# One mask product for both diagonal blocks of a bank of scores

## What is computed

```python
attn = jnp.einsum('bhqd,bhkd->bhqk', q, k) * scale
causal = jnp.triu(jnp.ones((Tc, Tc), dtype=bool), k=1)
attn = jnp.where(causal, -jnp.inf, attn)
attn = jax.nn.softmax(attn, axis=-1)
out = jnp.einsum('bhqk,bhkd->bhqd', attn, v)
```

```python
sim1 = jnp.einsum('bthd,hkd->bthk', q[..., 0, :], keys[:, :, 0, :])
s1, i1 = jax.lax.top_k(sim1, K)
fs, pk = jax.lax.top_k(all_sc, K)
hidden = jax.nn.gelu(jnp.einsum('btd,bthkd->bthk', xn, wd), approximate=False)
return jnp.einsum('bthk,bthkd->btd', hidden * jax.nn.relu(fs), wu)
```

## Time and profile before

| | us |
|---|---|
| median of 3 runs | 1625.49 |
| lowest and highest | 1624.69, 1626.40 |
| the profiled execution | 1626.17 |
| its span, first to last instruction | 1624.4 |
| granted TensorE clock, mean over the span | 0.904 |

### The profile page before, as it was taken

The page is one execution under the profiler, slowest core; times in us unless marked ns, Lnnn a source line. Parts: engine busy times, 40 slices in busy tenths (PEclk is TensorE's granted clock), DMA queues, the critical chain, the costliest instruction groups (busy, mean ns, idle before and its releaser), DMA issues.

```text
span 1624.4 us, 55167 instructions
## 1 busy us (share of the span) xinstructions
PE 1353.0 (83%) x21008; PEld 973.5 (60%) x21008; DVE 1358.7 (84%) x6568; ACT 926.0 (57%) x1502; POOL 665.0 (41%) x1024
## 2 busy tenths in 40 slices
PE   3567788989898998989898998989898988977567
PEld 3333456657575766667574766666575756655557
DVE  3314599999999898999999998999999998798984
ACT  0665766666675666666666766666666756442110
POOL 1412627171725436171826345270817355050410
PEclk9977899989898999989898999989898999998676
DMA  3000000000000000000000000000000000000000
GB/s 85 7 1 14 1 8 9 8 16 9 16 9 15 3 15 9 8 15 9 15 9 15 9 15 2 9 16 8 16 8 16 3 15 3 2 15 2 9 1 17
DMA packets 29989, 18.81 MB, mean 12 GB/s; under 512 B 1824, under 2 KB 29216, under 8 KB 29728
## 3 DMA queue, kind: packets, MB, share of 16 engines
q1 hardware_dynamic: 29728, 15.23, 3.3%
HBM read 11.04 MB, written 4.19 MB: 9 GB/s over the span
## 4 chain that ended last, share of the span: by engine, by line
PE 41%; DVE 36%; ACT 9%; issue 8%; POOL 5%; SPq 1%; DVEq 0%; DMA 0%; ACTq 0%; POOLq 0%
DVE onehot L1263 10%; PE G L938 7%; PE OV L827 7%; PE F L883 7%; DVE topi L1209 6%; PE G L927 6%; DVE psel L1225 4%; DVE whot L1288 3%; PE S L813 3%; DVE topv L1203 3%; ACT prob L631 3%; DVE fsel L1220 2%; DVE hid L1301 2%; PE S L753 2%; PE F L893 2%
## 5 line engine op out<-in xcount | busy, mean ns | idle before, releaser
L631 ACT ACTIVATE prob<-S 128x512 f32<-128x512 f32 x640 | 371.0, 596 | 146.7 <-PE S L815 140.4
L927 PE MATMUL G<-whot,onehot 128*128 128x16 bf16 x12288 | 383.5, 170 | 33.4 <-DVE hid L1301 19.6
L927 PEld LDWEIGHTS G<-whot,onehot 128*128 128x128 bf16 x12288 | 364.8, 97 | 68.2 <-issue 18.4
L1263 DVE TENSOR_TENSOR onehot<-lo_no,elo 128x1024 bf16<-128x1024 uint16 x512 | 386.4, 806 | 0.0
L827 PE MATMUL OV<-prob,vp 128*9 128x512 f32 (+3 forms) x2048 | 183.6, 508 | 67.9 <-ACT prob L631 62.0
L494 POOL TENSOR_TENSOR gat<-gat,cande 128x1280 f16<-128x1280 f16 x64 | 178.6, 2790 | 75.9 <-DVE gat L1231 75.9
L815 PE MATMUL S<-causal,ident_b 128*128 128x128 bf16 x1024 | 200.9, 229 | 0.0
L813 PE MATMUL S<-qT,kT_even 128*128 128x512 bf16 (+3 forms) x512 | 145.1, 312 | 53.7 <-ACT prob L631 45.0
L503 POOL COPY y<-y_new 128x512 f32<-128x512 f32 x16 | 9.8, 611 | 434.2 <-DVE r L1187 376.7
L563 ACT ACTIVATE hid<-F 128x512 f32<-128x512 f32 x128 | 76.6, 598 | 188.3 <-PE F L883 188.3
L827 PEld LDWEIGHTS OV<-prob,vp 128*9 128x9 f32 x2048 | 54.9, 99 | 198.2 <-issue 107.2
(11 more groups left out here) (134 smaller groups left out, 2498.7 us busy)
## 6 DMA issues: line engine op xcount, KB each, us to landing
xa<-in_L_attn_x SPq DMA_DIRECT2D x16, 256.0 KB, 2.9
xr<-in_L_attn_x SPq DMA_DIRECT2D x16, 256.0 KB, 3.0
out<-r SPq DMA_DIRECT2D x16, 256.0 KB, 2.3
onehot<-in_L_ffn_expert_down SPq DMA_DIRECT2D x1, 512.0 KB, 6.0
up<-in_L_ffn_expert_up SPq DMA_DIRECT2D x1, 512.0 KB, 6.6
onehot<-in_L_ffn_keys SPq DMA_DIRECT2D x1, 256.0 KB, 6.4
onehot<-in_L_attn_w_qkv SPq DMA_DIRECT2D x1, 192.0 KB, 4.4
onehot<-in_L_attn_w_proj SPq DMA_DIRECT2D x1, 64.0 KB, 4.7
```

Of the source, the lines that this page charges most:

```text
L631: act.activation(dst, src, ACT.Exp, scale=SCALE).then_inc(exp_done.sem, 1)
L927: last = nc.tensor.matmul(bank[:, 16 * i:16 * i + 16], onehot[:, row, :], whot[:, t, w_part, :], start=(w_part == 0), stop=(w_part == 2))
L1263: return dve.tensor_tensor(onehot[:, row:row + 8, :].rearrange("p t (c i) -> p t c i", i=2), lo, e, ALU.is_equal)
```

## The change

A unit with two blocks has one mask product where it had two. Both score products are issued first, and then one product of the identity with the mask, which is read twice (a step of 0 between the two readings), into the first 128 columns of both blocks (columns 0 and 256, or 0 and 384, of the bank). The second block's score product no longer has `start=True`. Units with one block keep their two products.

```diff
-                    for half, kc, col in SCORES[u % 5]:
+                    blocks = SCORES[u % 5]
+                    for half, kc, col in blocks:
+
                         pe_k = kT[half][:, j, kc * P:(kc + 1) * P]
                         nc.tensor.matmul(bank[:, col:col + T - kc * P], pe_k, qT[:, j, kc * P:T],
-                                         start=True, stop=False, skip_group_check=True)
-                        last = nc.tensor.matmul(bank[:, col:col + P], ident_b[:, :], causal[:, :],
-                                                start=False, stop=True, skip_group_check=True)
-                    last.then_inc(s_ready.sem, 1)
+                                         start=(col == 0), stop=False, skip_group_check=True)
+
+                    if len(blocks) == 2:
+                        diagonal = bank[:, :].rearrange("p (c n) -> p c n", n=P)[:, 0:NT:blocks[1][2] // P]
+                        mask = causal[:, :].unsqueeze(1).to_broadcast([P, 2, P])
+                    else:
+                        diagonal, mask = bank[:, 0:P], causal[:, :]
+                    nc.tensor.matmul(diagonal, ident_b[:, :], mask, start=False, stop=True, skip_group_check=True)\
+                        .then_inc(s_ready.sem, 1)
```

## The result

| | before | after |
|---|---|---|
| median, us | 1625.79 (4 runs) | 1649.70 (4 runs) |
| lowest and highest | 1624.69, 1626.40 | 1647.96, 1650.79 |
| ratio after to before | | 1.0147, 95% interval 1.0129 to 1.0164 |
| profiled execution, and its span | 1626.17, 1624.4 | 1648.66, 1646.9 |

The forecast was 1625.2 us in a range of 1620.5 to 1629.0. The kernel lost 24 us.

The account below looks back on a forecast made before the run. Neither PE nor DVE alone was taken to bound the kernel; they share the chain (41% and 36%). 128 merged masks on the chain at 2.5 ns save 0.3 us from the 1625.49 us median, giving 1625.2 us, range 1620.5 to 1629.

Parts of the forecast that it names:

- the part on the merged masks: PE's mask products in 384 two-block units: 384 products and 384 loads go, while the columns stay.
- Merged mask, 2.5 ns each, 0.3 us in all: Two-block units on the chain, 8 per iteration over sixteen iterations: 128 x 2.5 ns = 0.3 us less.
- The order and the start flag: First mask moved behind the second block's scores, and that score product with start=False: neither costs anything.
- ACT's waits: ACT waiting for the last mask's semaphore: 140.4 us in 254 of 640 cases, expected to stay near 140 us.
- The new form of the mask: Merged mask's repeated reading and split output: 0.11 us taken, bounded by 7 us won and 18 us lost.
- Rival A: PE's operand loads are partly exposed where the chain passes: up to 12.5 us less, 1613 us; chance 4%.
- the 81 ns per pair: Skill's spacing of load and product pairs at 128 columns: each merged pair saves 64 ns, 8 us less in all.
- Rival B: PE takes the merged mask's new form at half the rate: 14 us more, 1639 us; chance 10%.
- Its own sign: Rival B's mark in the profile after: a distance of 0.14 us or more behind a merged mask.
- Rival C, the clock's pattern: PE's clock falls at other moments in the iterations: 1620.6 or 1627.7 us; chance 7% faster, 2% slower.
- the forecast's sign of 90.0 to 90.7 us: Loop iterations should stay between these lengths; a move of 0.3 us or more would mean another clock pattern.
- The range's lower end: Rival C's fast end of 1620.6 us less the 0.3 us gain, some 1620.5 us.

Follow-up runs that it names:

- after_dead145: Changed kernel with 148 more instructions ahead of the loop, a branch over 145 never-executed semaphore increments: 1621.59 us, 0.9976 of the kernel before.
- order_alone: Kernel before with the change's product order and start flag, but still two masks of 128 columns per unit: 1621.65 us, 0.9993 of the kernel before.
- after_shift145: Changed kernel with 145 executed empty semaphore increments at the start of PE's list, none in the loop: 1625.69 us, 1.0026 of the kernel before.
- before_dead61: Kernel before, its masks untouched, shifted by 64 instructions that are never executed: 1636.39 us, 1.0065 of the kernel before.
- before_shift64: Kernel before, its products untouched, with 64 executed empty semaphore increments at the start of PE's list: 1630.62 us, 1.0052 of the kernel before.
- before_dead7: Kernel before, shifted by 10 instructions that are never executed: 1668.41 us, 1.0269 of the kernel before.
- after_dead253: Changed kernel shifted by 256 instructions in all that are never executed: 1648.21 us, 1.0136 of the kernel before.

## Why the prediction was wrong

**The step that failed** is the first sentence of the part on the merged masks and what was made of it: "384 products and 384 loads go" was priced by the time that they take in a stream. Their absence also moved everything behind them in the list, by 144 instructions at the loop's head and 192 at its back branch. The forecast put this at nothing, without a term or a reason for it, and called the clock the only way by which 0.3 us could grow. What the runs showed in its place: with the positions restored the merged mask costs nothing (0.9996), and with positions like the changed kernel's the untouched kernel is 0.5 to 1% slower. The missing term was 2.5 us at each of eleven back branches, 27.6 us in all, less what the exit no longer costs. That the positions are the cause is shown; how the fetch is timed is the theory.

**What a row could have told.** The chain before held "issue" at 8% of the span, and its longest piece at the loop's exit was 3.42 us ahead of the attention product, with 0.20 to 0.26 us at each back branch. I took these for a matter of the loop, not for a price that depends on how many instructions there are. The page before showed 16.4 KB per instruction transfer, and the count of instructions up to the branch can be had from a built program without a run. The stop right behind the exit said where an edge lies. Together these rows could have told that the branch would land early in a block, but not what that costs.

**Point by point.**
- *Merged mask, 2.5 ns each, 0.3 us in all*: right as far as it can be told. The unit still takes 0.33 us, and with the branch in its old place the whole is 0.9996 of before. The loop's eleven iterations, 994.55 us before, are as long in after_dead145:

```profile
sum 994.59, PE 869.70 PEld 639.56 DVE 919.90 ACT 636.86 POOL 464.15; mean PE 79.06 PEld 58.14 DVE 83.63 ACT 57.90 POOL 42.20
```

- *The order and the start flag, nothing*: right (order_alone).
- *ACT's waits*: 136.6 us in 247 cases in place of 140.4 in 254, as forecast.
- *The new form of the mask*, bounded between 7 us won and 18 lost and taken at 0.11 us: right, it costs what a plain product of 256 columns costs.
- *Rival A, and the 81 ns per pair that the Trainium skill gives at 128 columns* (TensorE: Matmul & The Clock Gate, section Back-to-back issue gap): nothing of it shows; the mask of a unit with one block still takes 0.05 to 0.06 us.
- *Rival B* (14 us, slower) had the right sign by the wrong mechanism. Its own sign, 0.14 us or more behind a merged mask, isn't there: 0.11 us in front of the one-hot products. In front of other products, whose operands or waits differ, I read 0.13 and 0.14 us here and there, and did not follow that up.
- *Rival C, the clock's pattern*: not the cause of the loss. Over the eleven iterations the mean granted clock is 0.94 before and after, while an iteration went from 90.41 to 92.92 us. That breaks the forecast's sign of 90.0 to 90.7 us without another pattern of the clock, a case for which it had no rival. The pattern does vary. after_shift145 and after_dead145 have the same loop at nearly the same place, starting some 7 us later in the one, and there its eleven iterations sum to

```profile
sum 989.61, PE 862.10 PEld 636.50 DVE 917.95 ACT 636.46 POOL 465.65; mean PE 78.37 PEld 57.86 DVE 83.45 ACT 57.86 POOL 42.33
```

5.0 us less. Eight of its iterations have a mean clock of 0.96 and three 0.94; of those of after_dead145 two have 0.96, four 0.94 and five 0.92. The two profiles come from two chips, on which the kernel before itself differs by 3.2 us, so the 5.0 us can't be put down to the late start. By the ratios, 1.0026 and 0.9976, the two kernels are 8.1 us apart where their first products are 9.3 us apart, and the rest is within the intervals. Single iterations can also leave the forecast's bounds: one in the profile of order_alone took 95.3 us at a granted clock of 0.89. What sets the pattern is open.
- *The range's lower end*, 1620.6 - 0.3, takes the gain off twice. It decides nothing here.

**The sum, redone.** First gap: 1.11 - 0.22 = 0.9 us; second: the attention product takes 3.45 where 2.34 would do, 1.1 us; together 2.0 us for the iteration shown, and 2.51 us are measured on average over eleven, whose second gaps are mostly longer (0.77 us on average, 0.51 here). Over all eleven the attention product takes 1.36 us more, so the two gaps make 2.25 of the 2.51 us, and I didn't trace the rest. 11 x 2.51 = 27.6 us in the loop.

## What to carry to other kernels

Where an engine runs a hardware loop longer than a block of instructions, removing or adding instructions anywhere ahead of its back branch is a second change, to the places of head and branch. Count them before and after, and when a small edit moves the time by far more than its instructions are worth, shift the loop by instructions that are never executed before explaining anything by the edit. A comparison of two versions is fair only when both loops stand equally well. All this was measured on one kernel, on PE's list and with a loop that carries the hint; other engines and loops without it were not tried.

## What the runs showed of the hardware

- Ten instructions that are never executed cost the kernel before 43 us (1.0269). With the back branch 8 instructions into its block the gap is 2.25 to 3.69 us, at 62 1.1 to 1.3 on average, at 106 about 0.5, at 207 to 254 0.2 to 0.3. With the head 45 or 49 instructions ahead of its block's end the code behind stalls a second time, which adds 0.9 to 1.7 us to the attention product; with 93 ahead (before_dead61, before_shift64) it doesn't.
- At the loop's exit it is reversed: 3.15 to 3.42 us with the branch at 254, 1.1 to 1.6 us at 207 to 210, none at 62.
- In before_dead7 a gap of PE of 3.28 us or more was followed by a slow attention product (3.74 to 4.46 us in place of 2.34) in seven of seven cases, one of 2.6 us or less in none of four. Shorter gaps can do it too: one of 1.52 us in before_shift64 and one of 1.96 in before_dead61 did, each once in eleven, with a granted clock of 0.57 or 0.58 behind it; two of 1.98 and 2.00 us in after_dead253 did not.
- An empty semaphore increment costs PE up to 0.16 us (145 took at most 23.08 us), three times a product of 128 columns with its load (0.055 us).
- A moving operand with a step of 0 and an output in two pieces of a bank run at the speed of one run of 256 columns, 0.11 us.
